# Loads moved from SP's DMA queue to ScalarE's, a store issued behind the next step's load, and a reordered last quad, in a fused cross-attention and FFN kernel

## What is computed

```python
hidden_states = jnp.concatenate([context, latents], axis=1)
q = (latents @ Wq).reshape(b, q_len, N_KV_HEADS, N_GROUPS, HEAD_DIM)
k = (hidden_states @ Wk).reshape(b, kv_len, N_KV_HEADS, HEAD_DIM)
v = (hidden_states @ Wv).reshape(b, kv_len, N_KV_HEADS, HEAD_DIM)
scores = jnp.einsum('bqhgd,bkhd->bhgqk', q, k) * scale
attn = jax.nn.softmax(scores.astype(jnp.float32), axis=-1)
x = x + jnp.einsum('bhgqk,bkhd->bqhgd', attn, v).reshape(...) @ Wo   # latents = layernorm(x)
routing = softmax(xf @ gate_w.T)                                     # xf = layernorm(x)
x = x + (xf * (routing @ in_channel_scale)) @ sign(weight).T * (routing @ out_channel_scale) + bias
```

## Time and profile before

| | |
|---|---|
| median of 3 runs | 743.09 us (742.22 to 744.78) |
| profiled execution | 741.45 us, span 739.6 us |
| TensorE busy | 684.2 us, 93% of the span |
| VectorE, ScalarE, GpSimd busy | 61%, 47%, 41% |
| mean granted TensorE clock | 0.984 |
| DMA moved | 144.70 MB, mean 196 GB/s |

### The profile page before, as it was taken

The page is one execution under the profiler, slowest core; times in us unless marked ns, Lnnn a source line. Parts: engine busy times, 40 slices in busy tenths (PEclk is TensorE's granted clock), DMA queues, the critical chain, the costliest instruction groups (busy, mean ns, idle before and its releaser), DMA issues.

```text
span 739.6 us, 10880 instructions
## 1 busy us (share of the span) xinstructions
PE 684.2 (93%) x3368; PEld 566.3 (77%) x3368; DVE 454.1 (61%) x735; ACT 349.4 (47%) x881; POOL 300.6 (41%) x259
## 2 busy tenths in 40 slices
PE   6999999989998899999988999999889999888785
PEld 4888888767887688888876878787778888777563
DVE  4652235547775576766755666675656778767554
ACT  3343324635464456545534554564346545645311
POOL 3243001623453235434423452372237422657764
PEclk9999999999999999999999999999989999999997
DMA  9566457776578886755987777558977675543311
GB/s 322 204 220 241 171 206 245 229 201 201 176 206 231 238 250 193 214 172 166 237 248 208 209 211 212 161 177 248 245 208 208 172 206 167 175 144 120 96 43 43
DMA packets 92941, 144.70 MB, mean 196 GB/s; under 512 B 17448, under 2 KB 50216, under 8 KB 91872
## 3 DMA queue, kind: packets, MB, share of 16 engines
q1 hardware_dynamic: 92896, 144.20, 65.0%
HBM read 91.60 MB, written 52.56 MB: 195 GB/s over the span
## 4 chain that ended last, share of the span: by engine, by line
issue 40%; PE 34%; POOL 19%; DVE 3%; DMA 2%; ACT 1%; SPq 0%; POOLq 0%; ACTq 0%; DVEq 0%
PE bank L1054 20%; POOL p_low L440 9%; PE bank L1168 7%; POOL wq_pair L448 3%; POOL wo_pair L454 3%; PE bank L1153 2%; POOL y L465 2%; PE bank L1244 1%; PE bank L1203 1%; DMA raw_a<-in_L_xattn_Wv 1%; PE bank L1195 1%; DVE stats L774 1%; DVE acc L871 1%; DMA p_low<-p_park 1%; PE bank L1063 1%
## 5 line engine op out<-in xcount | busy, mean ns | idle before, releaser
L440 POOL TENSOR_TENSOR p_low<-p_low,p_high 128x1024 fp32r<-128x1024 f32 x64 | 154.5, 2414 | 295.7 <-ACT p_high L531 295.6
L1168 PE MATMUL bank<-wo_pair,oT 128*128 128x512 f32 x768 | 190.5, 395 | 1.8 <-DVE oT L771 1.4
L1054 PE MATMUL bank<-xT,wq_pair 128*128 128x512 f32 x768 | 187.8, 395 | 0.0
L1054 PEld LDWEIGHTS bank<-xT,wq_pair 128*128 128x128 f32 x768 | 142.0, 190 | 27.8
L1168 PEld LDWEIGHTS bank<-wo_pair,oT 128*128 128x128 f32 x768 | 140.0, 189 | 29.0 <-issue 1.9
L531 ACT ACTIVATE oT<-bank 128x512 fp32r<-128x512 f32 x64 | 38.3, 598 | 201.4 <-DVE bank L879 201.4
L614 ACT ACTIVATE prob<-bank,nmax 128x256 f32<-128x256 f32 x256 | 118.8, 470 | 18.3 <-DVE nmax L849 17.9
L864 DVE STREAM_TRANSPOSE p_turned<-prob 128x512 f32<-128x512 f32 x128 | 91.1, 711 | 54.8 <-ACT prob L614 53.9
L1054 PEld LDWEIGHTS bank<-kg,qT 128*128 128x128 f32 x768 | 109.5, 191 | 10.6 <-DVE qT L842 0.9
L1054 PE MATMUL bank<-kg,qT 128*128 128x256 f32 x768 | 112.6, 284 | 0.7 <-DVE qT L842 0.7
L849 DVE TENSOR_REDUCE nmax<-bank 128x2 f32<-128x512 f32 x128 | 87.6, 685 | 33.8 <-PE bank L1054 33.7
(11 more groups left out here) (87 smaller groups left out, 601.2 us busy)
## 6 DMA issues: line engine op xcount, KB each, us to landing
p_park<-p_turned SPq DMA_DIRECT2D x64, 512.0 KB, 5.9
p_low<-p_park SPq DMA_DIRECT2D x256, 128.0 KB, 3.0
r_all<-r_park SPq DMA_DIRECT2D x64, 256.0 KB, 4.1
v_park<-v_stage SPq DMA_DIRECT2D x8, 1024.0 KB, 4.8
raw_a<-in_L_xattn_Wq SPq DMA_DIRECT2D x8, 1024.0 KB, 9.7
raw_b<-in_L_xattn_Wo SPq DMA_DIRECT2D x8, 1024.0 KB, 10.1
k_park<-k_stage SPq DMA_DIRECT2D x8, 1024.0 KB, 3.9
kg<-k_park SPq DMA_DIRECT2D x32, 256.0 KB, 5.8
```

Source lines behind the costliest of these rows:

```text
L440: nc.gpsimd.tensor_tensor(part, part.bitcast(fp32), p_high[:, :].rearrange("p i c q -> p (i c q)"), ALU.subtract).then_inc(p_lo, 1)
L1054: last = nc.tensor.matmul(dst, left(a, c), right(b, c), start=(n == 0), stop=(n == 3 * chunks - 1))
L1168: last = nc.tensor.matmul(wo_bank[:, :], oT[:, s, h, :], wo_pair[:, w, h, :], start=((s, w) == TERMS[0] and h == 0), stop=((s, w) == TERMS ...
```

## The change

Five edits. (1) SP's step issues the load of the probabilities of step t+1 first, then the stores of step t+2, then the load of the reciprocals of step t+1. (2) The load of the probabilities is one DMA in place of four; to that end the keys' order within a 128-block is changed where K is staged, so that partition p of the load holds row p. Before the loop SP issues the four late K and V loads behind the second store. (3) Inside the steps, K, V and the weights are issued by ScalarE, between the first half of the exponentials and `p_half`; the 1 MB weight loads are split into four of 256 KB, spread over steps 1, 5, 6 (Wo) and 2, 3, 4 (Wq, and in the last group the FFN's weight). (4) In the last quad `y_transpose(t - 1)` is TensorE's last instruction of the step, and `logits`, the router and what follows from them are done in the next step, with t - 2. (5) GpSimd's last-quad additions of FFN outputs stand in a slightly different order.

```diff
+                sp.dma_start(words(p_low[:, t % 2]).rearrange("p i c q -> p i (c q)"),
+                             p_park[t % 4].rearrange("i p e -> p i e")).then_inc(p_in[t % 2], 16)
+            def fetch_r(g, qd, t, first=False):
...
             def step(g, qd, t, last):
...
-                if ahead:
-                    park_p(*ahead)
...
-                if ahead:
-                    fetch_p(*ahead)
+                if not (final and t + 1 >= B):
+                    fetch_p(*step_after(g, qd, t, 1), first)
+                if not (final and t + LEAD - 1 >= B):
+                    park_p(*step_after(g, qd, t, LEAD - 1))
+                if not (final and t + 1 >= B):
+                    fetch_r(*step_after(g, qd, t, 1), first)
...
+            def loads(g, qd, t, last):
+                final = last and qd == QUADS - 1
+                if not final:
+                    for h in {1: (0, 1), 5: (2,), 6: (3,)}.get(t, ()):
+                        act.wait_ge(wo_lo, count(g, QH, qd, QH))
+                        load_wo(*quad_after(g, qd, 1), h)
+                    ng, nqd = quad_after(g, qd, 1)
+                    for c in {2: (0, 1), 3: (2,), 4: (3,)}.get(t, ()):
+                        act.wait_ge(wq_lo, count(ng, QH, nqd, QH))
+                        if last:
+                            act.dma_start(raw_a[:, c, :], ffn_w[c * P:(c + 1) * P, :]).then_inc(ffn_in, 16)
+                        else:
+                            load_wq(*quad_after(g, qd, 2), c)
+                if qd == QUADS - 1 and not last:
+                    for p in range(2):
+                        act.wait_ge(s_ready[p], steps(g, qd, t + 1))
+                    act.wait_ge(av_ready, steps(g, qd, t + 1))
+                    load_kv(g + 1, t)
...
                 exps(*ahead, 0)
+                loads(g, qd, t, last)
...
                     dve.wait_ge(ffn_in, 16 * HC)
```

More of the change, by code:

```diff
@@ L277, in _ @@
                     sp.wait_ge(wv_lo, HC)
-                    load_wq(0, 0)
+                    for c in range(HC):
+                        load_wq(0, 0, c)
             sp.wait_ge(wk_lo, HC)
-            load_wo(0, 0)
+            for h in range(QH):
+                load_wo(0, 0, h)
             sp.wait_ge(xt_ready, B)
@@ L291, in _ @@
             sp.wait_ge(wq_lo, HC)
-            load_wq(0, 1)
+            for c in range(HC):
+                load_wq(0, 1, c)
             for i in range(2):
@@ L326, in _ @@
                 load_kv(0, b)
[L327 to L331, removed]
+            park_p(0, 0, 0)
+            fetch_p(0, 0, 0, first=True)
+            fetch_r(0, 0, 0, first=True)
+            park_p(0, 0, 1)
+            for b in range(LEAD + 1, B):
                 load_kv(0, b)
@@ L335, in step @@
                 final = last and qd == QUADS - 1
-                ahead = None if final and t + LEAD - 1 >= B else step_after(g, qd, t, LEAD - 1)
-                if ahead:
-                    park_p(*ahead)
[L339 to L345, removed]
-                        sp.dma_start(raw_a[:, :, :], ffn_w.rearrange("(c p) n -> p c n", p=P)
-                                     ).then_inc(ffn_in, 16)
-                    else:
-                        load_wq(*quad_after(g, qd, 2))
-                if qd == QUADS - 1 and not last:
-                    for p in range(2):
-                        sp.wait_ge(s_ready[p], steps(g, qd, t + 1))
-                    sp.wait_ge(av_ready, steps(g, qd, t + 1))
-                    load_kv(g + 1, t)
-                if ahead:
-                    fetch_p(*ahead)
+                first = g == 0 and qd == 0 and t == 0
+                if not (final and t + 1 >= B):
[4 more added lines that the diff above has]
+                    fetch_r(*step_after(g, qd, t, 1), first)
             def group(g, last):
@@ L754, in _ @@
             group(G - 1, True)
[L756 to L763 removed]
+            for b in (B - 2, B - 1):
+                yt_copy(b)
+                gate_exp(b)
+                routet_copy(b)
+                oscale_copy(b)
+                z_half(b)
         @block.vector
@@ L1023, in _ @@
             group(G - 1, True)
+            gate_max(B - 2)
+            gate_route(B - 2)
             ffn_scale(B - 3)
+            ffn_norm(B - 1)
             z_make(B - 2)
             z_rest(B - 2)
-            ffn_norm(B - 1)
             gate_max(B - 1)
@@ L1308, in _ @@
             group(G - 1, True)
+            logits(B - 2)
+            ffn_product(B - 3)
             route_transpose(B - 2)
-            ffn_product(B - 3)
             channel_scales(B - 2)
```

111 lines of the change are left out of this document (56 added, 55 removed).

## The result

The changed kernel takes 714.05 us (median of four runs, 711.72 to 716.45), the one before on the same chip 742.65: a ratio of 0.9615, 95% interval 0.9571 to 0.9659. The ratios in this document leave out executions over 1.5% above the fastest of the same kernel, so they are not exactly the quotients of the medians given. The forecast was 718.5 in a range of 704 to 730. The time is inside, 4.5 us under the point, but that it came so near is in part luck: several terms behind it were wrong and made up for each other, as the stretches show.

The account below looks back on a forecast made before the run. TensorE, busy for 93% of the span, was taken as the bound, with 35.1 us lost over seven quads. From 741.45 us: less 7.8, 11.3, 1.9 and 3.1, plus 1.2, gave 718.5, range 704 to 730.

Parts of the forecast that it names:

- First quad: First quad: one step stays about 1.2 us late, the other loss goes; 7.8 us gained, bounds 5 to 9.
- KV quads: Three KV quads: 21.8 us of stalls go, 10.5 come back through ScalarE's issues and late loads; 11.3 gained.
- Nothing for all three: SP's order, the single load of the probabilities and K's new key order: no gain from any.
- a queue that mostly waits: SP's queue: one issue in place of four saves 1.3 us, but the load still waits for its store.
- the reading of the stall: KV quads: the probabilities' load waits for its store, then queues behind K and V; TensorE waited 1.01 us.
- The rule on queues: KV quads: a second issuer saves only issue time if DMA engines are full; rival at 726.0 us, chance 0.17.
- ScalarE's issues: ScalarE in KV quads: 0.6 us per DMA issue, of which 3.2 us a quad exceed the cover.
- Other quads: The two remaining quads: stalls on `p_high` go, 1.9 of 4.3 us gained, bounds 0 to 4.
- The FFN's weight: Quad 7 of 8, step 4: VectorE waits for the last weight piece; 1.2 us lost once, bounds 0 to 3.
- Last quad without its step 0: Last quad and tail: y waits go, router waits come; net 3.1 us gained, bounds 3 lost to 9 gained.
- VectorE's router operation ending with the GpSimd operation beside it: Last quad: the router operation takes 1.19 us in place of a few tenths, so the router comes at about 6.5.
- The wait of 2.2 us: Last quad's steps: TensorE waits 2.2 us for the router, 1.5 where half of the scores fill part.

Follow-up runs that it names:

- the repeated run: The changed kernel, unaltered, run again with the third group of experiments: 713.51 us, ratio 0.9644 to the kernel before.
- the moved operation: The changed kernel with VectorE's two sign operations per step of the seventh quad moved behind the accumulation: 708.67 us, ratio 0.9617.
- the last version: The changed kernel with all loads on SP, sign operations later, FFN pieces earlier, and step 2's router transpose later in the last quad: 702.06 us, ratio 0.9497.

## Why the prediction was right, and where it was not

**First quad, forecast 7.8 gained.** 6.4 in the profiled execution, in the lower half of its bounds, but its first two steps vary between executions of the same kernel: the repeated run lost 3.0 us more there (71.85, a gain of 3.4, outside the bounds), about half of it in the second step, at a granted clock of 0.85. The traces of all runs split the gain: with four loads in the old order the quad takes 74.5 to 75.3 us, with the single load in the old order 72.1 to 73.7, with the single load in the new one 68.8 to 71.9. So the new order helps, as forecast, and a part is the single load's, priced at nothing.

**KV quads, forecast 11.3 gained, measured 21.4.** Two steps failed. "Nothing for all three", said of SP's order and the single load, left out the transfer itself: a load in four parts of 32 partitions takes 0.65 us more of all 16 DMA engines. It also took SP for "a queue that mostly waits", for which the 1.3 us of issues could not matter. The second step was the reading of the stall: "the store of the probabilities is issued at 509.74, K and V behind it, the load must wait until the store has landed". The load for which ScalarE waited at 515.97 had been issued earlier, as these rows of the kernel before show:

```profile
500.40 0.38 SPq L302 DMA_DIRECT2D p_park<-p_turned  x1
...
507.17 1.99 SPq L315 DMA_DIRECT2D p_low<-p_park  x4
...
520.26 0.38 SPq L302 DMA_DIRECT2D p_park<-p_turned  x1
```

It stood ahead of the store at 509.74 and of that step's K and V in the queue, and still 8.8 us passed from its first issue to `p_high`. The same view shows what SP did: it stored at 509.74, could issue the next load only at 517.94, 8.2 us later, and came to its next store at 520.26. That is 10.5 us from store to store, where a step has 8.28, of which it waited 5.6 for the store's landing and none for anything else. With the single load in the same order SP went from store to store in 8.26 to 8.30 us throughout the three KV quads, and at the worst place that I read (store issued at 364.11 with a weight, K and V behind it, load at 370.33, `p_high` at 377.31) ScalarE waited 0.66 us and TensorE not at all. So the single load alone is enough to empty the KV quads, and four loads across all partitions nearly are (67.43, 66.24, 66.33).

How the narrow loads made the steps long is read from rows and not tested. Full DMA engines are not it by the mean share alone: a quad ran without a stall at 0.88 with all loads on SP, and the stalled ones of the kernel before had 0.83 to 0.85. And no run has the new order or the second queue with the four narrow loads, so whether either would have emptied the KV quads without the single load, as the prediction in part assumed, stays open.

**The rule on queues.** The prediction set a rule of the Trainium skill ("DMA: Bandwidth & Descriptors", Issuing engines are not separate DMA queues) against the gain and kept both. The runs agree with the rule: 713.15 us with SP alone, 714.05 with two issuers.

**ScalarE's issues, forecast 0.6 us each.** Their median is 0.34 us. They mostly run beside an exponential and cost 0.1 to 0.2 us a KV quad, 0.1 to 1.0 in the repeated run. The worst one stands right behind SP's issue of the large load (at 289.41), and holds `p_high` back by 1.91:

```profile
290.24 0.34 ACTq L685 DMA_DIRECT2D raw_a<-in_L_xattn_Wq  x1
...
290.75 2.08 ACTq L685 DMA_DIRECT2D raw_a<-in_L_xattn_Wq  x1
...
292.95 1.06 ACT L523 ACTIVATE p_high<-p_low 128x1024 fp32r<-128x1024 f32 x1 [1.91 <-issue]
```

**Other quads, forecast 1.9 gained, measured 0.1.** The stalls on `p_high` went, and such issues and the loop's first steps took their place. In the repeated run it was 1.0.

**The FFN's weight, forecast 1.2 lost, measured 7.2** (3.1 and 4.1). That the last piece lands late was the step, and it is nearly without effect; the collision of VectorE and GpSimd is the cause of the 3.1, shown by the moved operation. Of the 4.1 in step 0, 1.6 are the granted clock of 0.87, which the repeated run did not have. That the two operations meet because the load is on time is read from rows, and holds only in part. The run with the single load alone has the same 68.95 and 13.33, but both runs with four loads collide too, where their loads are on time, and leads of 0.20 and 0.04 us in the kernel before are not the load's doing.

**Last quad without its step 0, forecast 3.1 gained, measured 8.4.** Step 7 came out at 10.18 where I said 10.3. The forecast of 11.3, 11.3 and 10.8 for steps 3 to 5 failed at "VectorE's router operation ending with the GpSimd operation beside it": they take 10.02, 10.09 and 9.22, because beside the normalisation it is not held up. Step 3 and the tail of the changed kernel:

```profile
646.16 2.10 POOL L457 TENSOR_SCALAR y<-acc,mv,rstd 128x512 f32<-128x512 f32 x1 [0.18 <-POOL rstd L404]
647.30 0.23 DVE L975 SCALAR_TENSOR_TENSOR route<-gexp,grec,route 128x8 fp32r<-128x8 f32 x1
647.58 0.33 PE L1245 MATMUL bank<-ident,route 128*128 128x128 f32 x1 [0.28 <-DVE route L975]
...
697.05 2.53 POOL L418 TENSOR_TENSOR acc<-acc,bias_b 128x512 f32<-128x512 f32 x2
698.40 1.20 DVE L975 SCALAR_TENSOR_TENSOR route<-gexp,grec,route 128x8 fp32r<-128x8 f32 x1
```

The earlier trace rows showed it beside an addition of two tensors, and I carried that over to an operation with one. The wait of 2.2 us that I expected in each step came in step 2 alone (2.47), where no FFN product stands ahead of the transpose; TensorE's clock then fell to half and the step took 3.4 us more. The tail got 1.3 us shorter, not 1.0 longer, at a granted clock of 0.89 where it had 0.77, so part of that is the clock and not the order.

Five errors, then: 10.1 and 5.3 us too little gain forecast (KV quads, last quad), and 1.4, 1.8 and 6.0 too much gain or too little loss (first quad, other quads, FFN's weight). Their sum is -6.2; with 0.6 ahead of the first quad that is the 6.8 us between the forecast's 22.9 and the traces' 29.7. Had only the errors of one sign been made, the time would have been off by 15 or by 9 us.

## What to carry to other kernels

Before pricing an edit of a DMA by its issues, price the transfer: the same bytes to 32 partitions at a time kept all DMA engines busy 0.65 us longer than to 128, and in this kernel's old order, with the DMA engines busy for 0.83 to 0.85 of the time, undoing that alone removed nearly all of the stall. When a late transfer is named by a wait, find the row in which it was issued before saying what it queued behind. And where an edit makes one engine earlier, look which VectorE and GpSimd operations with two SBUF tiles then start together: 0.06 us decided whether a VectorE operation took 0.69 or 2.88 us, and the step 8.28 or 9.6.

## What the runs showed of the hardware

A VectorE operation with two SBUF inputs that started 0.06 us behind a two-tensor operation of GpSimd took 2.88 us instead of 0.69, and ended 0.55 us after it. Where VectorE started 0.04 us ahead (629.92 in the kernel before), it took its 0.69 and GpSimd's operation 2.93 instead of 2.40. Beside a GpSimd operation with one tensor input (2.10 us) the small router operation took its usual 0.23, in all four steps in which the two overlapped. The Trainium skill ("SBUF — State Buffer", Who interferes with whom) says that a VectorE instruction with two SBUF inputs contends with a GpSimd instruction that reads SBUF, that the lock is exclusive, and that issue order decides who blocks. The rows agree for two tensors and not for one.

The first sign operation, which reads one SBUF tile, was held too: at 577.13 in the changed kernel, 0.61 us behind `p_rest`, it took 2.07 us instead of 0.39.

TensorE's granted clock was 0.75 over the step with the wait of 2.47 us (634.93), with six products of the scores taking 1.63 us there and 0.96 elsewhere, so for a part of the step at 1.2 GHz of 2.4, and 0.87 over step 0 with waits of 1.11 and 2.90 us. The length of a wait does not settle it: the same waits left step 0 of the repeated run at 1.00, and in the kernel before a wait of 2.53 us in step 2 (655.96) did too. In the last version, with step 0 at 9.24 us and step 2's wait at 1.78, it stayed at 1.00 in both, and step 2 was 2.8 us shorter than in the changed kernel on the same chip (13.40 at 0.75).
